# A cross-attention and mixture-of-experts kernel on one core: low parts and combination weights change engines, gathers and scatter-adds change order, late loads go one by one, maybe-empty tiles are nested

## What is computed

```python
# x [8,256,512], ctx [8,256,512], mask [8,256]; 8 experts of width 192, top 2 per token
def reference(x, ctx_2048, mask_BxS2_bk0, g_xattn, g_ffn, w_router, w_gate, w_up, w_down):
    x = x + tanh(g_xattn[0]) * xattn(layernorm(x), ctx_2048, mask_BxS2_bk0)
    return x + tanh(g_ffn[0]) * ffn(layernorm(x), w_router, w_gate, w_up, w_down)

def xattn(h, mem, mask):                     # scores = h mem^T / sqrt(512), softmax, times mem
    ...
def ffn(x, w_router, w_gate, w_up, w_down):
    probs = softmax(xt @ w_router.T)
    top_v, top_i = top_k(probs, 2); top_v = top_v / sum(top_v)
    comb = zeros((T, 8)).at[arange(T)[:, None], top_i].add(top_v)
    g = einsum('th,eih->tei', xt, w_gate); u = einsum('th,eih->tei', xt, w_up)
    return einsum('tei,ehi,te->th', silu(g) * u, w_down, comb)
```

## Time and profile before

| | us |
|---|---|
| median of 3 runs | 287.52 |
| lowest and highest of the 3 | 286.6, 290.8 |
| the profiled execution, its own time | 286.73 |
| span of the profiled execution | 284.8 |

### The profile page before, as it was taken

The page is one execution under the profiler, slowest core; times in us unless marked ns, Lnnn a source line. Parts: engine busy times, 40 slices in busy tenths (PEclk is TensorE's granted clock), DMA queues, the critical chain, the costliest instruction groups (busy, mean ns, idle before and its releaser), DMA issues. The chain is left out here.

```text
span 284.8 us, 5700 instructions
## 1 busy us (share of the span) xinstructions
PE 245.1 (86%) x1514; PEld 215.2 (76%) x1514; DVE 176.5 (62%) x595; ACT 145.2 (51%) x326; POOL 157.1 (55%) x183
## 2 busy tenths in 40 slices
PE   8999998999999889999989949999999999992300
PEld 8898886877778768887978838888889999991200
DVE  5457999998998988665655534665666664442000
ACT  3557755557574636365555524565556654442000
POOL 2455656657463562663375484865774875748030
PEclk9999999999999999999999997999999999997555
DMA  5997999999876383479595598785874886949230
GB/s 177 371 361 238 339 293 304 309 293 286 269 226 193 108 241 131 56 196 322 125 282 109 107 276 205 124 172 119 145 129 102 148 159 100 173 96 163 68 75 0
DMA packets 30866, 54.02 MB, mean 190 GB/s; under 512 B 5360, under 2 KB 9584, under 8 KB 30832
## 3 DMA queue, kind: packets, MB, share of 16 engines
q0 software_dynamic: 8544, 20.62, 37.0%
q1 hardware_dynamic: 22288, 32.98, 35.6%
HBM read 34.64 MB, written 18.95 MB: 188 GB/s over the span
## 5 line engine op out<-in xcount | busy, mean ns | idle before, releaser
L510 POOL DMA_INDIRECT out<-YT,IXI x36 | 59.6, 1655 | 56.9 <-issue 23.2
L1286 PE MATMUL S<-WGh,XTb 128*128 x144 | 52.0, 361 | 0.4 <-ACT XTb L673 0.4
L489 POOL DMA_INDIRECT XG<-x2s,IXI x42 | 42.0, 999 | 13.1 <-issue 12.1
L1287 PE MATMUL S<-WGl,XTb 128*128 x144 | 48.7, 338 | 0.0
L694 ACT ACTIVATE YT<-PV,cj 128x512 f32<-128x512 f32 x36 | 24.8, 689 | 31.3 <-PE PV L1324 31.3
L997 DVE TENSOR_TENSOR XTb<-A,XTb 128x512 fp32r<-128x512 f32 x37 | 25.6, 691 | 16.6 <-ACT XTb L673 16.5
L1149 PE MATMUL PV<-CX,PT 128*128 128x260 f32 x128 | 31.7, 390 | 3.0 <-ACT PT L600 2.9
L1136 PE MATMUL S<-CT,XLT 128*128 128x264 f32 x128 | 31.1, 386 | 0.0
L1292 PE MATMUL S<-WGh,XTb 128*128 x144 | 31.1, 338 | 0.0
L680 ACT ACTIVATE SG<-S 128x192 f32<-128x192 f32 x36 | 11.9, 331 | 37.6 <-PE S L1292 37.6
L438 POOL TENSOR_TENSOR rs<-mv,CS 128x1 f32<-128x1 f32 x32 | 17.8, 557 | 23.9 <-DVE mv L769 23.4
(11 more groups left out here) (156 smaller groups left out, 498.5 us busy)
## 6 DMA issues: line engine op xcount, KB each, us to landing
WGl<-in_wgu SPq DMA_DIRECT2D x24, 256.0 KB, 5.1
X<-in_x SPq DMA_DIRECT2D x16, 256.0 KB, 4.9
CT<-in_ctxt SPq DMA_DIRECT2D x8, 512.0 KB, 6.4
CX<-in_ctxn SPq DMA_DIRECT2D x8, 512.0 KB, 5.4
out<-X SPq DMA_DIRECT2D x16, 256.0 KB, 4.2
x2s<-Y SPq DMA_DIRECT2D x16, 256.0 KB, 5.2
WD1l<-in_wd SPq DMA_DIRECT2D x8, 256.0 KB, 5.9
WS<-in_wd SPq DMA_DIRECT2D x8, 256.0 KB, 4.6
```

The costliest lines, as they stand in the source:

```text
L489: pool.indirect_dma_start(out=XG[:, j % NX, :], out_offset=None, in_=known, in_offset=bass.IndirectOffsetOnAxis(ap=IXI[:, j:j + 1], axis=0))\
L510: pool.indirect_dma_start(out=out, out_offset=bass.IndirectOffsetOnAxis(ap=IXI[:, j:j + 1], axis=0), in_=YT[:, j % NB, :], in_offset=None, ...
L1286: pe.matmul(o, XTh[:, j % 2, c, :], WGh[:, e, c, :], start=(c == 0), stop=False)
L1287: pe.matmul(o, XTh[:, j % 2, c, :], WGl[:, e, c, :], start=False, stop=False)
```

## The change

Five things change.

1. The low parts of the first 15 units move from GpSimd to VectorE: lo(u) now runs at the end of VectorE's step, for the units of the step before; the last one runs after the loop, ahead of Tsb.
2. coefs of batches 0 to 5 moves from VectorE to GpSimd, at the end of its odd steps, with a wait after two of its instructions (step). VectorE's ranks waits for comb of the batch before. coefs of batches 6 and 7 stay. norm moves from the end of a step into the next step.
3. In GpSimd's tile loop gather(j + 6) stands ahead of scatter(j).
4. From unit 22 on, a weight load waits until the one before has landed.
5. Dead tiles: on each engine groups of four nested Ifs take the place of single ones (filled). The end is found by halving (ending) on TensorE, ScalarE and GpSimd, and GpSimd waits there first for the unread gathers, then for the scatter-adds.

```diff
+        def filled(eng, n, first, tile):
+            for j in range(first, NF):
+                tile(j)
+            for g in range(NF, NT, 4):
+                with ExitStack() as nest:
+                    for j in range(g, min(g + 4, NT)):
+                        nest.enter_context(eng.If(n > j - NE))
+                        tile(j)
+        def ending(eng, n, end, a=NF, b=NT):
+            if a == b:
+                end(a)
+                return
+            m = (a + b + 1) // 2
+            with eng.If(n > m - 1 - NE):
+                ending(eng, n, end, m, b)
+            with eng.Else():
+                ending(eng, n, end, a, m - 1)
...
# SyncE, loadw(u)
+                if u > PRE + MORE:
+                    sp.wait_ge(*loaded(u - 1))
...
# GpSimd
-            def lo(u):
...
+            def step(ins):
+                steps[0] += 1
+                ins.then_inc(s_pd, 1)
+                pool.wait_ge(s_pd, steps[0])
+            def coefs(b):
+                pool.wait_ge(s_e2, 2 * b + 2)
+                pool.wait_ge(s_ms, b + 1)
+                pool.tensor_scalar(cc[:, :, 0:1], e2[:, :, :], -0.5, 0.5, ALU.mult, ALU.add)
+                step(pool.tensor_scalar(cc[:, :, 1:2], e2[:, :, :], 0.5, 0.5, ALU.mult, ALU.add))
+                step(pool.tensor_tensor(out=pc[:, :, :, :], in0=OH[:, :, :, :],
+                                        in1=cc[:, :, :].unsqueeze(3).to_broadcast([128, 2, 2, E]), op=ALU.mult))
+                pool.tensor_tensor(out=comb[:, 2 * b:2 * b + 2, :], in0=pc[:, :, 0, :], in1=pc[:, :, 1, :],
+                                   op=ALU.add).then_inc(s_cb, 1)
...
-                for u in units(s - 1):
-                    if s >= 3:
-                        pool.wait_ge(s_pv, s - 2)
-                    lo(u)
...
+                if s >= 5 and s % 2 == 1:
+                    coefs((s - 5) // 2)
...
-            for j in range(4, NT):
-                with lives(pool, live, j):
-                    scatter(j)
-                    if j + NX < NT:
-                        gather(j + NX)
-            landed(NF)
...
+            def tile(j):
+                if j + NX < NT:
+                    gather(j + NX)
+                scatter(j)
+            def end(n):
+                for j in range(n, min(n + NX, NT)):
                     pool.wait_ge(s_g[j % NX], 16 * (j // NX + 1))
+                landed(n)
+            filled(pool, live, 4, tile)
+            ending(pool, live, end)
...
# ScalarE (TensorE alike, with down in place of yev)
+            filled(act, live, NE, tile)
+            ending(act, live, lambda n: yev(n - 1))
...
# VectorE
             def ranks(b):
                 dve.wait_ge(s_lc, b + 1)
+                if b:
+                    dve.wait_ge(s_cb, b)
...
-                main, side, after = [], [], []
+                main, side, after = [], [norm(s - 2)], []
...
-                    side.append(coefs((s - 5) // 2))
...
-                after.append(norm(s - 1))
                 run(braid(queue(*main), queue(*side)))
                 run(rowmax(s - 1))
                 run(*after)
+                for u in units(s - 1):
+                    lo(u)
...
+            for u in units(2 * B - 1):
+                lo(u)
             dve.wait_ge(s_tab, RB)
             dve.tensor_copy(Tsb[:, :], PTB[:, 0:128]).then_inc(s_tse, 1)
```

## The result

The changed kernel takes 272.19 us (median of 4 runs, 271.77 to 273.60) against 288.91 us before (median of 4). The ratio is 0.943, 95% interval [0.934, 0.952]. The profiled execution took 271.77 us with a span of 270.0 us; before it was 286.73 and 284.8. A run of 276.12 us (x_skip) and one of 284.42 us (x_both) further down are in the slower of two states that executions show; they stand in the medians and ranges, and not in the ratios.

The account below looks back on a forecast made before the run. TensorE and VectorE nearly fill the attention stage; TensorE paces the later tiles, the first nine stall on gathers. From 286.73 us, -2.25 - 7.3 - 2.3 - 2.0 = -13.85 gives 273 us, range 266 to 280.

Parts of the forecast that it names:

- Attention stage, -2.25 forecast: Attention stage: low parts to VectorE and coefs to GpSimd gain 3.5 us, less 1.25 us at Tsb; bounds -3.8 and +1.25.
- VectorE sits out that instruction: Attention stage: VectorE's long operations come from waiting out a whole GpSimd subtraction of a low part, 1273 ns.
- the 12.8 us: VectorE's total loss beside 15 GpSimd subtractions of low parts, some 10.2 us of it expected to go.
- The bound of 3.8 us: Attention stage: most that could be won, TensorE's idle time, since it is busy 57.02 of 60.80 us.
- The price of Tsb, 1.25 us: End of attention stage: two subtractions ahead of Tsb start it 1.25 us late, and TensorE's L1220 waits for it.
- Rival (a): Attention stage gains nothing: VectorE's twelve new subtractions wait for GpSimd's small operations, 6.7 us; total 276.5 us; chance 0.16.
- First half of the tiles, -7.3 forecast: First nine tiles: gathers ahead of scatter-adds end TensorE's waits for gathers, gaining 7.3 us; bounds 4.0 and 7.3.
- rival (c): Tile stage: weight loads one by one come late; 285 us at 5.7 us a load, 300 at 6.5; chance 0.08.
- TensorE's branch walk, -2.3 forecast: After the last full tile: nested groups and halving shorten TensorE's walk by 2.3 us; bounds +0.6 and -5.2.
- drop seven short ones: Branch walk: seven short branches go at about 0.27 us each, 1.9 us, and 0.4 more for two not taken.
- I leave two long ones: Branch walk: the two long branches, 5.94 us of the 8.42, were assumed to remain.
- The tail, -2.0 forecast: Kernel end: GpSimd's drain begins sooner after the last scatter-add, with fewer checks, gaining 2.0 us; bounds 0 and 2.7.

Follow-up runs that it names:

- x_skip: Changed kernel with the gathers of tiles that nobody reads left out on GpSimd; 270.65 us, ratio to before 0.936.
- x_both: Changed kernel with the scatter-add ahead of the gather again and the waits between late weight loads taken out; 281.92 us, ratio to before 0.979.
- x_engines_back: Changed kernel with low parts of the first 15 units back on GpSimd and coefs back on VectorE, norm left moved; 272.21 us, ratio to before 0.950.
- x_low_gpsimd: Changed kernel with the low parts of the first 15 units back on GpSimd, coefs staying there too; 272.69 us, ratio to before 0.948.
- x_scatter_first: Changed kernel with the scatter-add ahead of the gather again, loads still one by one; 276.98 us, ratio to before 0.962.
- x_coefs_vector: Changed kernel with coefs of batches 0 to 5 back on VectorE, low parts staying on VectorE; 274.25 us, ratio to before 0.948.
- x_burst: Changed kernel with the waits between late weight loads taken out, gathers still ahead of scatter-adds; 273.90 us, ratio to before 0.954.
- x_flat: Changed kernel with single Ifs in place of nested groups and 13 Ifs in a row in place of the halving; 273.00 us, ratio to before 0.950.
- x_when: Changed kernel with the last low parts run a step or two earlier, so none stands ahead of Tsb; 272.30 us, ratio to before 0.942.
- x_inline: Changed kernel with the last down and last Y in an equality If ahead of each maybe-empty tile; 274.43 us, ratio to before 0.954.

## Why the prediction was right, point by point

The forecast was 273 us, from a profiled execution of 286.73; the changed kernel's profiled execution took 271.77. The sum of the forecast was -13.85 us, and the profiles differ by 14.96. The terms:

**Attention stage, -2.25 forecast, -2.18 measured** from the start of the span to the first XTb copy: -4.64 in the loop, +1.38 at Tsb, +0.28 behind it, and +0.81 ahead of the first value product, whose start varies from 15.0 to 16.6 us over the profiles of these kernels. That the sum comes out is in part luck: the loop gave more than the 3.5 us that were taken, and the late start, which no edit explains, took the excess back. The reason is not complete either. "VectorE sits out that instruction" is borne out: the long operations are real, and the moves end them. What is not borne out is that the 12.8 us had to go for the loop to shorten: x_engines_back keeps more than half of that loss and has the same loop. What was left out of the sum is norm: the change lists it, and the forecast gave it no price. With norm alone most of VectorE's 2.6 us of waits go, some 5 us less are lost beside GpSimd, and that brings VectorE under TensorE. The rows for it stood in the trace before: VectorE's waits for e and P.

The bound of 3.8 us at this step was too low as well. It took TensorE's busy time as fixed (57.02 of 60.80), but the same number of matmuls, 345, is busy for 52.65 us before and 50.97 in x_engines_back, both at a granted clock of 1.00. Busy time as the profile counts it was no floor here; where the 1.68 us went is not shown (the profile models the ends of matmuls).

The price of Tsb, 1.25 us, was right: TensorE waits 1.51 us at L1250 and the stretch is 1.38 us longer. It is paid for low parts on VectorE, and since x_low_gpsimd and x_engines_back have the short loop without it, this move costs more in these stretches than it gives; the medians are too close to tell.

The bounds for coefs on GpSimd were 1.1 and 3.7 us, and 1.27 was measured. Rival (a), twelve subtractions that wait on VectorE, fell: L960 takes 0.69 us beside those operations. It is GpSimd that is held up: its L489 takes 193 ns in the median, and 634 where it starts beside a subtraction of VectorE. On the rule that was weighed here, from the Trainium skill, "SBUF — State Buffer", section "Who interferes with whom": these runs show long VectorE operations where GpSimd runs subtractions of 1.27 us, and none beside operations of 0.3 us, which agrees with the lock that the section describes, held for a whole instruction.

**First half of the tiles, -7.3 forecast, -7.59 measured.** The mechanism is as forecast: x_scatter_first and x_both show the stalls of 2.0 and 3.96 us when the gather stands behind the scatter-add. Over the ten kernels with both edits the gain is 5.6 to 7.8 us, since a stall can still come (2.43 us in x_coefs_vector). The forecast counted the loads one by one at no cost and no gain; with the new order no gain stands clear of the spread (1.14 us in x_burst), with the old one they give 3.67 us. The period of the loads, forecast at 3.5 to 4.5 us, is 4.05, and rival (c), late loads, fell.

**TensorE's branch walk, -2.3 forecast, -1.57 measured.** TensorE's idle time before the last down is the two long branches and the rest: 5.94 + 2.48 = 8.42 us before, 6.56 + 0.28 = 6.84 after, 3.89 + 2.28 = 6.17 in x_flat, which has as many branches as before. The rest is 0.28 us in each of the nine kernels that find the end by halving on TensorE. So "drop seven short ones" is right, 2.2 us against the forecast's 2.3. What was mis-sized is the other half of that step, "I leave two long ones", which took their length for fixed: two were kept, but each takes 1.36 to 4.66 us over the profiles, and a pair 5.50 to 7.92 us in the nine kernels. In the walk as a whole (9.65 to 12.08 us in the nine, 10.04 in x_flat, 12.29 before) the gain is hidden by that spread. Whether nesting and halving make the long ones longer is open: there are only two pairs without them, 5.94 and 3.89 us.

**The tail, -2.0 forecast, -2.13 measured.** The drain begins 5.19 us after the last scatter-add and lasts as long as before. In the five other kernels with the same end on GpSimd and the last scatter-add waiting for TensorE's walk (x_burst, x_low_gpsimd, x_coefs_vector, x_engines_back, x_when) it is 5.12 to 5.91 us, so the gain is 1.4 to 2.2. x_flat gives about 1.2 us of it to GpSimd's branches, and x_scatter_first and x_both (6.29 and 6.48 us) 0.4 to 1.4 to the order; these overlap, since a check that ends before the scatter-add has landed costs nothing.

**The second half of the tiles, 0 forecast, -1.23 measured.** Over the profiles of these kernels the same stretch takes 78.84 to 80.74 us, and 80.07 before lies within. No gain is shown here; the pair of profiles happens to differ.

## What to carry to other kernels

A change that moves several things should be priced for each of them, the small reordering too: where an engine with little slack waits for another at the end of its step, moving that wait one step later can be worth as much as moving work to another engine. Before a long instruction is blamed, ask which waits the loop has beside it, and undo the parts both singly and together. Undone one at a time, an edit can look idle because another one covers for it (here the loads one by one, which the order of the gathers covers for), and only undoing both engine moves together showed that norm is enough. When a wait is as long as the sum of a few long pieces, split it before judging an edit: the halving's 2.2 us on TensorE show only with the two long branches set apart. A wait that is removed shows what it was hiding (here GpSimd's lag behind TensorE's walk).

## What the runs showed of the hardware

GpSimd's drain at the end goes with the number of indirect DMAs it issued: 78 of them (36 scatter-adds and 42 gathers) give 6445 ns, 73 give 6037, that is 82.6 and 82.7 ns each (one kernel of the eleven with 78 took 6.51 us; three have 73). Leaving out five unread gathers shortens the drain by 0.41 us.

The branch instructions differ by engine: on ScalarE and GpSimd the branches of the end take 34 to 53 ns, on TensorE 68 to 239 (one of 366 before, one of 459 with x_inline's edit), but for two in each execution with 1.4 to 4.7 us (one, of 2.8 to 3.9, with x_inline's edit). The Trainium skill, "Runtime: NRT & Kernel Launch", section "Instruction fetch mechanics", says that a taken branch whose target lies outside the window waits for a fetch; the long ones would fit that, but no run here shows where the targets lie, nor why the same branch takes 3.3 us in one profile and 4.7 in another (L359, x_low_gpsimd and x_scatter_first).

TensorE's granted clock falls while it walks: from 252.4 us on it is at half in the changed kernel, the 1.2 GHz level; TensorE had run no matmul since 247.0. The products of the last down take 0.63 us each where those of the tile before took 0.39.
